# Local-attention layers on one core: the order of each half step re-arranged on five engines

## The reference

```python
def attn_layer(x, Wqkv, qs, ksc, Wo):
    q, k, v = jnp.split(x @ Wqkv, 3, -1)       # 16 heads of 64
    q = l2norm(q) * qs
    k = l2norm(k) * ksc
    q = q * cos * scale + rotate_half(q) * sin * scale
    k = k * cos * inv + rotate_half(k) * sin * inv
    out = local_attention(q, k, v)             # windows of 32 queries, 64 keys, masked softmax
    return out.transpose(0, 2, 1, 3).reshape(b, n, INNER) @ Wo

for i in range(6):
    x = attn_layer(shift_tokens(x), Wqkv[i], q_scale[i], k_scale[i], Wo[i]) + x
    x = ffn_layer(shift_tokens(x), ln_g[i], ln_b[i], W1[i], b1[i], W2[i], b2[i]) + x
```

## Time and profile before

| | |
|---|---|
| runs | 3875.07 us median of 3 (3874.39 to 3875.17) |
| the profiled execution | 3872.81 us; span 3871.0 us |
| mean granted clock of TensorE | 0.971 |
| busy, us of the span | TensorE 3542.8, weight loads 2679.4, VectorE 2948.5, ScalarE 3021.4, GpSimd 2494.8 |

### The profile page before, as it was taken

The page is one execution under the profiler, slowest core; times in us unless marked ns, Lnnn a source line. Parts: engine busy times, 40 slices in busy tenths (PEclk is TensorE's granted clock), DMA queues, the critical chain, the costliest instruction groups (busy, mean ns, idle before and its releaser), DMA issues.

```text
span 3871.0 us, 95171 instructions
## 1 busy us (share of the span) xinstructions
PE 3542.8 (92%) x30888; PEld 2679.4 (69%) x30894; DVE 2948.5 (76%) x4344; ACT 3021.4 (78%) x6096; POOL 2494.8 (64%) x2313
## 2 busy tenths in 40 slices
PE   5898679999889999889999899999799999799998
PEld 3444357777567777577777577776577777577776
DVE  4666378886788886788886788886788886788876
ACT  3556478887688887688887698886688886788885
POOL 3555377775377774577773577773677772677762
PEclk8999799999999999999999899999899999899999
DMA  4223200000100000000001000001000001000002
GB/s 134 86 91 94 55 2 1 0 0 1 30 2 0 0 0 22 9 2 0 0 0 30 2 2 0 0 0 30 2 1 0 0 1 29 2 1 0 0 1 72
DMA packets 59745, 67.76 MB, mean 18 GB/s; under 512 B 12006, under 2 KB 40164, under 8 KB 58468
## 3 DMA queue, kind: packets, MB, share of 16 engines
q1 hardware_dynamic: 59492, 64.64, 5.8%
HBM read 46.27 MB, written 18.35 MB: 17 GB/s over the span
## 4 chain that ended last, share of the span: by engine, by line
ACT 37%; issue 25%; PE 21%; DVE 12%; ACTq 2%; POOL 2%; DMA 1%; SPq 0%; DVEq 0%; POOLq 0%
PE bank L401 18%; ACT sb_area L790 18%; ACT bank L790 5%; DVE sb_area L1280 4%; ACT sb_area L940 4%; DVE sb_smax L1277 4%; ACT sb_lnb L952 3%; ACT sb_lnb L949 3%; ACT sb_area L983 2%; PE bank L673 1%; DVE sb_area L1155 1%; DVE sb_area L1257 1%; PE bank L614 1%; DVE sb_ssq L1267 1%; DMA sb_wqk_lo<-qk_rows 1%
## 5 line engine op out<-in xcount | busy, mean ns | idle before, releaser
L790 ACT ACTIVATE sb_area<-bank 128x512 f32<-128x512 f32 (+4 forms) x2149 | 1335.2, 648 | 209.4 <-PE bank L401 154.9
L1257 DVE TENSOR_TENSOR sb_area<-bank,sb_rots 128x1024 f32<-128x1024 f32 x768 | 939.1, 1225 | 393.7 <-ACT sb_area L940 392.9
L1520 POOL TENSOR_TENSOR sb_area<-sb_area,sb_rn 128x512 f32<-128x512 f32 x768 | 785.7, 1044 | 586.3 <-ACT sb_rn L956 586.3
L401 PE MATMUL bank<-sb_area 128*64 128x64 f32 (+6 forms) x17104 | 1062.2, 275 | 21.2 <-ACT bank L790 8.7
L1506 POOL TENSOR_TENSOR sb_area<-sb_area 128x512 f32<-128x512 f32 x768 | 969.4, 1280 | 86.6 <-DVE sb_area L1257 84.8
L401 PEld LDWEIGHTS bank<-sb_area 128*64 128x64 f32 (+4 forms) x17104 | 746.9, 145 | 283.1 <-issue 229.5
L401 PE MATMUL bank<-sb_wqk_hi,sb_xwin 128*128 128x512 f32 x1536 | 723.6, 473 | 55.7 <-DVE sb_xwin L1237 47.6
L401 PE MATMUL bank<-sb_area,sb_wvo 128*128 128x256 f32 x3072 | 728.3, 381 | 3.1 <-DVE sb_xT L1312 3.1
L401 PEld LDWEIGHTS bank<-sb_area,sb_wvo 128*128 128x128 f32 x3072 | 555.0, 190 | 78.4 <-issue 12.8
L614 PE MATMUL bank<-sb_ident,sb_area 128*128 128x128 f32 x3072 | 488.4, 282 | 39.9 <-ACT sb_area L790 31.2
L614 PEld LDWEIGHTS bank<-sb_ident,sb_area 128*128 128x128 f32 x3072 | 354.6, 143 | 235.6 <-issue 124.8
(11 more groups left out here) (115 smaller groups left out, 3979.4 us busy)
## 6 DMA issues: line engine op xcount, KB each, us to landing
qk_rows<-sb_p SPq DMA_DIRECT2D x52, 256.0 KB, 4.2
sb_wqk_hi<-qk_rows SPq DMA_DIRECT2D x32, 256.0 KB, 2.9
sb_wqk_lo<-qk_rows SPq DMA_DIRECT2D x32, 256.0 KB, 2.7
sb_area<-in_Wqkv SPq DMA_DIRECT2D x7, 1024.0 KB, 6.1
sb_area<-in_WvT SPq DMA_DIRECT2D x7, 512.0 KB, 7.4
sb_wo_bd<-in_Wo SPq DMA_DIRECT2D x14, 256.0 KB, 8.3
sb_area<-in_x SPq DMA_DIRECT2D x4, 512.0 KB, 6.1
sb_area<-in_x SPq DMA_DIRECT2D x8, 256.0 KB, 2.9
```

What stands on the lines that cost most here:

```text
L401: return nc.tensor.matmul(o, a, b, start=start, stop=stop, skip_group_check=True)
L790: return nc.scalar.activation(o, i, ACT.Copy)
L1257: tt_(t12[:, c % 2, :, :].rearrange("p u (h d) -> p u h d", h=8), src, bc(rots[:, tt, s, :, :], [P, 2, 8, D], 2), ALU.mult).then_inc(S["ro ...
L1520: pt_(qn[:, c, :].rearrange("p (h d) -> p h d", h=8), qsum[:, c % 2, :].rearrange("p (h d) -> p h d", h=8), r, ALU.mult).then_inc(S["qn"], 1)
```

## The change

All functions stay; their order within the half changes on four engines, with the waits and buffers that this needs.

- TensorE: the transposes `turn_qk(2wp)` come first, then both projections, directly behind them the scores, then `turn_p`, `weigh`, and the windows (now in the second half) between `weigh` and `turn_qk(2wp + 1)`.
- ScalarE: the mask comes first and waits for `sub` itself; both squares stand together; `exp` and `norms` stand behind them and handle the half before; `turned_p`, `weighed`, the windows' copy (second half) or the token heads (first half), and `turned_qk(2wp + 1)` end the half.
- VectorE: `sums` stand behind the rotations. GpSimd: the first `add` stands ahead of the scale multiplications.
- Squares have four buffers in place of two; `add` writes into `qn` itself, where it wrote into `qsum`, and `scale` works in place.

```diff
-        sqb, t12 = take(2, 512), take(2, 2, 512)
-        qsum, qn = take(2, 512), take(4, 512)
+        sqb, t12 = take(4, 512), take(2, 2, 512)
+        qn = take(4, 512)
...
-                        if c == 1:
+                        if c == 3:
                             pe.wait_ge(S["xwev"], g_of(bt) * 4 + tt + 1)
                         else:
                             pe.wait_ge(S["ev"], g)
...
-                        pe.wait_ge(S["ev"], g * 4 + 1)
+                        pe.wait_ge(S["ev"], g * 4 + 3)
...
                     for wp in range(2):
+                        turn_qk(2 * wp)
                         project(2 * wp)
-                        turn_qk(2 * wp)
-                        turn_p(wp)
                         project(2 * wp + 1)
                         score(wp)
-                        if wp == 0:
+                        turn_p(wp)
+                        weigh(4 - wp, 1 - wp)
+                        if wp == 1:
                             windows()
-                        weigh(4 - wp, 1 - wp)
                         turn_qk(2 * wp + 1)
                         project_out(wp)
...
-                        act.wait_ge(S["ssq_raw"], g)
-                        nc.scalar.activation(sqb[:, c % 2, :], pj[c % 2][:, :], ACT.Square).then_inc(S["sq"], 1)
...
+                        act.wait_ge(S["ssq_raw"], g + 1 - c % 2)
+                        nc.scalar.activation(sqb[:, c, :], pj[c % 2][:, :], ACT.Square).then_inc(S["sq"], 1)
...
+                        act.wait_ge(S["sub"], g_of(bt) * 8 + 2 * tt + wp + 1)
+                        first = tt == TT - 1 and wp == 1
                         copy(sbank[:, :], lmask[:, 0 if first else 1, :]).then_inc(S["masked"], 1)
...
                     for wp in range(2):
+                        mask_ahead(3 - wp, 1 - wp)
+                        turned_qk(2 * wp)
                         square(2 * wp)
-                        turned_qk(2 * wp)
+                        square(2 * wp + 1)
+                        exp(3 - wp, 1 - wp)
+                        norms(1 - wp, 1 - wp)
                         turned_p(wp)
-                        square(2 * wp + 1)
-                        if wp == 0:
+                        weighed(4 - wp, 1 - wp)
+                        if wp == 1:
                             windows()
-                            if not (part == 0 and t == 0) and (v := behind(t, i, part, -1)):
-                                heads_of_tokens(*v)
-                        weighed(4 - wp, 1 - wp)
+                        elif not (part == 0 and t == 0) and (v := behind(t, i, part, -1)):
+                            heads_of_tokens(*v)
                         turned_qk(2 * wp + 1)
-                        exp(wp)
-                        mask_ahead(wp)
-                        norms(wp)
...
                     for wp in range(2):
-                        sums(3 - wp, 1 - wp)
                         rotate(2 * wp)
                         rotate(2 * wp + 1)
+                        sums(3 - wp, 1 - wp)
                         shift(wp)
...
-                        pool.wait_ge(S["qn"], g + 5)
+                        pool.wait_ge(S["tr"], g)
...
                     for wp in range(2):
-
+                        add(2 * wp)
                         scale(1 - wp, 2 - 2 * wp)
                         scale(1 - wp, 3 - 2 * wp)
                         normalise(3 - wp, 1 - wp)
-                        add(2 * wp)
                         add(2 * wp + 1)
```

More of the change, by code:

```diff
@@ L938, in square, with norms @@
                         act.wait_ge(S["proj"], g + 1)
-                        act.wait_ge(S["ssq_raw"], g)
-                        nc.scalar.activation(sqb[:, c % 2, :], pj[c % 2][:, :], ACT.Square).then_inc(S["sq"], 1)
-                    def norms(half):
-                        if not (v := behind(t, i, part, 0)):
+                        act.wait_ge(S["ssq_raw"], g + 1 - c % 2)
+                        nc.scalar.activation(sqb[:, c, :], pj[c % 2][:, :], ACT.Square).then_inc(S["sq"], 1)
+                    def norms(lag, half):
+                        if not (v := behind(t, i, part, lag)):
                             return
@@ L947, in norms @@
                         n = (g_of(bt) * 4 + tt) * 2 + half
-                        act.wait_ge(S["ssq_raw"], 2 * n + 3)
+                        act.wait_ge(S["ssq_raw"], 2 * n + 5)
                         nc.scalar.activation(lnb[:, tt % 2, half, :], ssq[:, tt % 2, half, :], ACT.Relu,
@@ L976, in turned_qk, with exp @@
                         m.then_inc(S["ev"], 1)
-                    def exp(wp):
-                        if not (v := behind(t, i, part, 2)):
+                    def exp(lag, wp):
+                        if not (v := behind(t, i, part, lag)):
                             return
@@ L983, in exp, with mask_ahead @@
                         nc.scalar.activation(dd[:, wp, :], dd[:, wp, :], ACT.Exp).then_inc(S["exp"], 1)
-                    def mask_ahead(wp):
-                        if not (v := behind(t, i, part, 2)):
+                    def mask_ahead(lag, wp):
+                        if not (v := behind(t, i, part, lag)):
                             return
-                        first = v[0] == TT - 1 and wp == 1
+                        tt, bt = v
+                        act.wait_ge(S["sub"], g_of(bt) * 8 + 2 * tt + wp + 1)
+                        first = tt == TT - 1 and wp == 1
                         copy(sbank[:, :], lmask[:, 0 if first else 1, :]).then_inc(S["masked"], 1)
@@ L1109, in _ @@
             column = iter(range(28))
-            for name, n in (("sq", 1), ("rotd", 1), ("ssq_raw", 1), ("add", 1), ("tr", 3), ("score", 2), ("yy", 2),
+            for name, n in (("sq", 1), ("rotd", 1), ("ssq_raw", 3), ("add", 1), ("tr", 3), ("score", 2), ("yy", 2),
                             ("pt", 2), ("qn", 6), ("ln_part", 3), ("pn", 1), ("oo", 1)):
@@ L1266, in square_sums @@
                         dve.wait_ge(S["ln_part"], g_of(bt) * 8 + 2 * tt + half)
-                        nc.vector.tensor_reduce(ssq[:, tt % 2, half, :], sqb.rearrange("p c (h d) -> p (c h) d", h=8), AX.X, ALU.add)\
+                        nc.vector.tensor_reduce(ssq[:, tt % 2, half, :], sqb[:, 2 * half:2 * half + 2, :].rearrange("p c (h d) -> p (c h) d", h=8), AX.X, ALU.add)\
                             .then_inc(S["ssq_raw"], 2)
@@ L1502, in add @@
                         g = g_of(bt) * 16 + (4 * tt + c)
-                        pool.wait_ge(S["qn"], g + 5)
+                        pool.wait_ge(S["tr"], g)
                         pool.wait_ge(S["rotd"], g + 2)
                         swapped = t12[:, c % 2, 1, :].rearrange("p (h e d) -> p h e d", h=8, e=2)[:, :, ::-1, :]
-                        pt_(qsum[:, c % 2, :].rearrange("p (h e d) -> p h e d", h=8, e=2),
+                        pt_(qn[:, c, :].rearrange("p (h e d) -> p h e d", h=8, e=2),
                             t12[:, c % 2, 0, :].rearrange("p (h e d) -> p h e d", h=8, e=2), swapped, ALU.add)\
@@ L1517, in scale @@
                         pool.wait_ge(S["add"], g + 2)
-                        pool.wait_ge(S["tr"], g)
                         r = rn[:, tt % 2, half, 8 * (c % 2):8 * (c % 2) + 8].unsqueeze(2).to_broadcast([P, 8, D])
-                        pt_(qn[:, c, :].rearrange("p (h d) -> p h d", h=8),
-                            qsum[:, c % 2, :].rearrange("p (h d) -> p h d", h=8), r, ALU.mult).then_inc(S["qn"], 1)
+                        sums_of_heads = qn[:, c, :].rearrange("p (h d) -> p h d", h=8)
+                        pt_(sums_of_heads, sums_of_heads, r, ALU.mult).then_inc(S["qn"], 1)
                     def normalise(lag, wp):
```

## The result

The changed kernel takes 4160.32 us in the median (4152.87 to 4163.79, 4 runs) against 3874.73 for the kernel before: 1.0736 times, with a 95% interval of 1.0718 to 1.0755. It is slower by some 286 us; 4137 was forecast, with a range of 4050 to 4210.

What follows compares the result with a forecast made beforehand. TensorE's own order was taken to bind within some 2% of a ScalarE-VectorE ring; two new waits add 1.69 us a step: 6 x (27 x 1.69 - 2.0) = 262 us, giving 4137 us, range 4050 to 4210.

Steps and rivals of the forecast that it cites:

- the ring: Waits between ScalarE and VectorE, from squares through rotation, maximum and subtraction to exponential; ScalarE 37%, VectorE 12% of the chain.
- TensorE alone: TensorE's own blocks in a step if nothing waits: 6.96 us plus 7.18, sum 14.14, against 14.16 now.
- The first rival: TensorE's spacing is elastic, so the new waits vanish and ScalarE's work limits: 1.50 us less a step, 3632; chance 0.05.
- The wait in half B: Second half (wp = 1): turn_qk(3) waits for ScalarE's windows' copy behind weighed; TensorE stands 1.24 us, half 8.42.
- The wait in half A: First half (wp = 0): turn_qk(2) waits for turned_qk(1) to copy out rbank; TensorE stands 0.47 us, half 7.43.
- One of ScalarE's terms: Token heads on ScalarE in the first half, between weighed and the turned_qk(1) copies: 0.37 us.
- The step: One token tile, both halves: 7.43 + 8.42 = 15.85 us against 14.16, +1.69 us.
- Fill and drain: Start and end of each layer, outside steps 5 to 31: -2.0 us a layer together, chosen between -4 and 0.
- the norms stand in the middle of the next half: GpSimd's scale can begin at about 4.3 in the first half, 3.1 us before its block is due; costed at nothing.
- The later ring: Rival: norms or sums in their new place make GpSimd or VectorE late by 0.25 us each half: 4218, chance 0.14.
- the sign named for it: A wait for GpSimd's scale before TensorE's transposes would show the fourth rival, the later ring.

Runs made afterwards that it cites:

- e10: e7 with turn_p and the windows ahead of the scores on TensorE: 3792.15 us, 0.9791 of the kernel before.
- e7: e5 with GpSimd's two scale multiplications ahead of the first add again: 3821.15 us.
- e5: Changed kernel with windows transposed behind the scores and copied ahead of turned_p, and in the first half turned_qk(1) copied out ahead of weighed: 3841.17 us.
- e1: Changed kernel with the windows put back ahead of weighing on TensorE, and copied ahead of turned_p and weighed on ScalarE: 3905.79 us.
- e2: Kernel before with only the windows moved, transposed behind weighing and copied behind weighed in the first half: 4015.94 us.
- e4: Changed kernel with turned_qk(1) copied out ahead of weighed on ScalarE in the first half: 4080.71 us.
- e9: Changed kernel with half of the output projection left out (two of every four heads; the output lacks them): 4007.30 us.
- e8: Changed kernel with GpSimd's two scale multiplications ahead of the first add again: 4138.15 us.
- e3: Changed kernel with the norms directly behind the mask on ScalarE: 4217.06 us.

## Why the prediction was right

**What bounds the kernel.** That TensorE was as full as the ring, so that cutting the ring alone would bring next to nothing, holds: with both waits removed the step is 14.02 us (forecast for TensorE alone 14.14, before 14.22) and TensorE is busy for 100 of 100 us. That its blocks are the limit there, e10 bears out: another order on TensorE alone shortens the step of e7, which is also 14.02. The busy share of TensorE's weight loads told of no slack that could be used: it was 78.57 of 100 us before, and in e5, where TensorE has no gap, it is 79.61. The first rival, elastic blocks, is excluded by e5, and by the changed kernel itself: after a wait the blocks run at the same spacing (output to transposes 1.73 us, at 731.55 and in the earlier trace rows).

**The wait in half B.** Forecast 1.24 us; 1.05 to 1.23 were measured, and half B is 8.50 us in the mean against 8.42. e1 removes it, e2 makes it in the kernel before.

**The wait in half A.** Forecast 0.47 us, measured 2.09 - 1.73 = 0.36. One of ScalarE's terms was too long: the token heads take 0.20 to the next copy (739.01 to 739.21 in the trace of the changed kernel), not 0.37. e4 removes the wait, and e9 shows that ScalarE sets the half.

**The step.** Forecast +1.69, measured +1.52. The 14.16 that I subtracted is a step without the turn of the loop; the mean is 14.22, because the first of four steps took 14.5. In the changed kernel the steady steps lie between 15.67 and 15.83 us, and the turn of the loop adds nothing that stands out.

**Fill and drain, the term that was mis-sized.** I took -2.0 us a layer, between -4 and 0. Measured is 47.93 - 27 x 1.52 = +6.9, outside those bounds. Two causes are shown. The step "the norms stand in the middle of the next half: the scale multiplications on GpSimd can begin at about 4.3" left out that `add` had moved ahead of scale on GpSimd; that is hidden in a full step, but not in the short ones of the fill: e8 takes 3.0 us a layer off (530.43 against 533.45). And I counted the waits for the copies only from step 5, where the fill has them too: in e5, without them, the same difference is 481.15 - 485.52 + 27 x 0.20 = +1.0. With both causes taken away, in e7, a layer takes 477.2 us and the difference is -2.9, within the bounds that I had set. The errors of step and fill had opposite signs, so the sum is nearer than its terms: 262 forecast, 286 measured.

**The later ring** of the fourth case did not come in the steady steps; the sign named for it, a wait for GpSimd's scale before the transposes, came in the fill alone (3.50 and 2.21 us). What would have made it is shown by e3, where ScalarE is late by a few tenths, and by e10, where VectorE is.

## What to carry to other kernels

When a ring of waits between two engines is cut, lay out the third engine's own blocks first: if they fill the step already, the cut gives next to nothing (here 0.20 of 14.22 us) and every new wait on that engine counts in full. For a bank that several producers share, look in each engine's order for what stands between a use and the copy that frees it; here an instruction of 1024 columns was put ahead of a copy of 256, and the block behind it in TensorE's order could no longer cover it. Moving that copy back, and one more ahead of the large one, made the new order faster than the old, by some 0.9% (e5).

## What was not expected of the hardware

VectorE's small operations between on-chip tiles became up to six times longer, with nothing changed in them. `rests_of_tile`, which subtracts two tiles, took 0.28 us in the kernel before and 1.12 in the changed one (medians of 192; least, median and most in ns):

```profile
L1237 DVE TENSOR_TENSOR sb_xwin<-sb_xs,sb_xwin x192: 279/282/540, 485.6 to 3730.4; 128x128 fp32r<-128x128 f32 x192
```

```profile
L1239 DVE TENSOR_TENSOR sb_xwin<-sb_xs,sb_xwin x192: 280/1115/1437, 489.3 to 4016.9; 128x128 fp32r<-128x128 f32 x192
```

The token copies of 0.22 us took up to 1.36. One of them, and the GpSimd operation under which it began:

```profile
732.59 1.21 DVE L1232 COPY sb_xs<-sb_xT 64x128 f32 x1
```

```profile
732.39 1.32 POOL L1508 TENSOR_TENSOR sb_area<-sb_area 128x512 f32<-128x512 f32 x1
```

The copy ends at 733.80, within 0.1 us of the end of the GpSimd operation at 733.71. The traces tell the cases apart. In the changed kernel 180 of the 192 subtractions began while a GpSimd operation ran, and their median is 1.12 us; the 12 others took 0.29 each. In the kernel before, 6 began so, with 0.54 us, and the other 186 took 0.28 to 0.30. VectorE's operations that read a result bank took the same in both. So the new order puts these small operations under GpSimd's work, and VectorE's busy time in a step rises from 12.1 us (85.34% of 14.22) to 13.4 (85.09% of 15.74).

The Trainium skill, in "GPSIMD Engine Reference", section "1. Specifications", says that GpSimd's interfaces to the on-chip memory are shared with VectorE, and that instructions of VectorE with two inputs there, or in a two-port mode, contend. The rows agree in the two-input case, the subtraction; that the copy runs in such a mode no row here says. In the changed kernel this lies off TensorE's path; in e10, with VectorE busy 98.42 of 100 us, it may be part of what the step lacks.
